# A graph network on one core: the row-by-row tile in five steps of sixteen instead of one of four, and the loads of the node windows addressed in bytes

## The reference

```
h = x @ enc_W + enc_b
for l in range(3):
    cat = concat([h[src], h[dst], edge_attr_16])
    m = relu(cat @ msg_W1[l] + msg_b1[l]) @ msg_W2[l] + msg_b2[l]
    agg = segment_sum(m, dst, num_segments=12500)
    h = gru_cell(agg, h, ...)
out = layernorm(x + relu(h @ ro_W1 + ro_b1) @ ro_W2 + ro_b2)
```

## Time and profile before

| what | value |
|---|---|
| runs of the kernel | 9832.15, 9768.75, 9798.1 us; median 9798.1 |
| the profiled execution's own time | 9777.42 us |
| its span from first to last instruction | 9775.6 us |
| busy: POOL / DVE / PE / ACT | 4639.2 / 3532.6 / 2880.1 / 346.4 us |
| granted TensorE clock, mean | 0.571 of full speed |
| rows issued one by one at L473 | 9792 on SP, 9792 on ACT |
| gathers at L798 | 4767 (and 63 more at other lines) |

### The profile page before, as it was taken

One profiled execution on the slowest core, in us unless ns is written; L12 is line 12 of the kernel. 1 busy time (PEld: TensorE's weight loads), 2 busy tenths in 40 slices (PEclk: granted clock), 3 DMA queues, 4 the chain that ended last, 5 costly groups with the idle time before them and its releaser, 6 DMA issues.

```text
span 9775.6 us, 72182 instructions
## 1 busy us (share of the span) xinstructions
PE 2880.1 (29%) x7290; PEld 1610.2 (16%) x7290; DVE 3532.6 (36%) x4656; ACT 346.4 (4%) x542; POOL 4639.2 (47%) x4865
## 2 busy tenths in 40 slices
PE   3323322322322332222222222223232222322223
PEld 2111111111111221111111111112111111111112
DVE  2333333333333433333333333333333334333334
ACT  0000000000000000000000000000000000000001
POOL 5444444444444454444444444445454445545543
PEclk6555555555555555555555555555555555555555
DMA  3111111111111111111111111111111111111111
GB/s 87 31 31 30 30 30 30 28 31 30 31 30 30 30 28 30 30 30 30 30 30 29 30 30 27 30 31 30 30 31 31 30 30 34 31 31 31 31 30 25
DMA packets 351443, 308.63 MB, mean 32 GB/s; under 512 B 149364, under 2 KB 237518, under 8 KB 350568
## 3 DMA queue, kind: packets, MB, share of 16 engines
q0 software_dynamic: 155328, 159.79, 8.6%
q1 hardware_dynamic: 118271, 110.17, 4.0%
q10 hardware_dynamic: 77328, 33.96, 1.4%
HBM read 280.52 MB, written 22.83 MB: 31 GB/s over the span
## 4 chain that ended last, share of the span: by engine, by line
SPq 57%; issue 38%; DVE 2%; PE 1%; another core or an unknown queue 1%; DMA 0%; ACT 0%; POOL 0%; DVEq 0%; ACTq 0%; POOLq 0%
SPq L473 46%; SPq L469 6%; SPq L642 2%; SPq L633 1%; SPq L527 1%; DVE work_ps L1493 1%; SPq L630 1%; DVE folds L1528 0%; DVE p_src L1490 0%; PE bank L838 0%; DMA p_src<-p_tab 0%; PE work_ps L949 0%; PE bank L962 0%; SPq L662 0%
## 5 line engine op out<-in xcount | busy, mean ns | idle before, releaser
L798 POOL DMA_INDIRECT p_src<-p_tab,idx_all x4767 | 4551.1, 955 | 4916.8 <-DVE work_ps L1493 3467.4
L962 PE MATMUL bank<-hot,folds 128*128 128x96 f32 x2496 | 660.1, 413 | 4012.9 <-issue 2053.0
L1490 DVE TENSOR_TENSOR p_src<-work_ps,p_src 128x512 f32<-128x512 f32 x624 | 427.6, 685 | 3374.9 <-DMA p_src<-p_tab 2912.1
L962 PEld LDWEIGHTS bank<-hot,folds 128*128 128x128 f32 x2496 | 532.1, 296 | 4278.5 <-issue 2198.0
L949 PE MATMUL work_ps<-w_edges,msg 128*128 128x512 f32 x1248 | 1120.0, 997 | 21.4 <-DMA windows_sb<-q_tab 21.4
L1523 DVE SCALAR_TENSOR_TENSOR work_ps<-work_ps,rel 128x1024 f32<-128x1024 f32 x624 | 768.8, 1232 | 21.5
L1493 DVE TENSOR_TENSOR work_ps<-p_src,bank 128x1024 f32<-128x1024 f32 x624 | 767.0, 1229 | 21.4
L1528 DVE TENSOR_REDUCE folds<-work_ps 128x256 f32<-128x1024 f32 x624 | 758.4, 1215 | 0.0
L959 PE MATMUL bank<-hot,counts 128*34 128x96 bf16 x416 | 68.9, 261 | 2248.6 <-issue 1278.6
L1538 DVE TENSOR_TENSOR sums<-bank,sums 128x96 f32 x624 | 158.1, 253 | 872.6 <-remote 699.5
L959 PEld LDWEIGHTS bank<-hot,counts 128*34 128x34 bf16 x416 | 27.1, 108 | 2368.2 <-issue 1359.8
(11 more groups left out here) (167 smaller groups left out, 1800.9 us busy)
## 6 DMA issues: line engine op xcount, KB each, us to landing
p_src<-p_tab ACTq DMA_DIRECT2D x9792, 0.2 KB
p_src<-p_tab SPq DMA_DIRECT2D x9792, 0.2 KB
p_src<-p_tab,idx_all POOLq DMA_INDIRECT x4830
msg<-in_edge_k SPq DMA_DIRECT2D x156, 256.0 KB
pick<-rel_tab SPq DMA_DIRECT2D x312, 96.0 KB
windows_sb<-q_tab ACTq DMA_DIRECT2D x312, 24.0 KB
windows_sb<-q_tab SPq DMA_DIRECT2D x312, 24.0 KB
pick<-q_tab ACTq DMA_DIRECT2D x312, 24.0 KB
```

Of the source, the lines that this page charges most:

```text
L798: pool.indirect_dma_start(out=p_src[r][0:rows, t, :], out_offset=None, in_=p_tab[l][0:NODES, :], in_offset=bass.IndirectOffsetOnAxis(ap=id ...
L962: last = nc.tensor.matmul(fold_ps, folds[:, b, :], hot_all[n % 2][:, s * BLOCKS + b, 1:WINDOW + 1], start=(b == 0), stop=(b == BLOCKS - 1))
L1490: nc.vector.tensor_tensor(rows, edge_ps[k % 2], rows, ALU.add).then_inc(with_edge, 1)
```

## The change

What it does, in four parts. (1) `SINGLE_STEPS` lists the steps whose last tile is loaded row by row, in all layers alike: of every 16 steps those with m % 16 in (3, 6, 9, 12, 15), without the last step, 64 a layer. POOL gathers 7 tiles there. (2) Rows on SP and ACT are issued in pieces of 16, ordered by a due time `max(5 * m - 25 + 4 * q, 0)` in fifths of a step (there are 64 entries, so `every` is 4): SP puts the pieces due before 5(4g-6) ahead of the inputs of group g, ACT those due in [5m, 5m+5) at step m. (3) In layer 0 the shift of a chunk's counts and the load of chunk nodes come one group later, behind the first piece of rows of that group. (4) DVE makes byte offsets of the window starts once (two small operations before the first step), SP and ACT load those, and a window's address needs no register operation.

```diff
+SINGLE_STEPS = [[m for m in range(STEPS - 1) if m % 16 in (3, 6, 9, 12, 15)]] * LAYERS
+SINGLE_ROWS = SINGLE_STEPS[0]
+SINGLES = len(SINGLE_ROWS)
...
-        def has_singles(m):
+        def has_singles(l, m):
 
-            return m % GROUP == GROUP - 1 and m // GROUP < SINGLES
+            return m in SINGLE_STEPS[l]
...
-        def pieces_at(m):
-
-            due = [(m + AHEAD_OF - q, q) for q in range(PIECES)]
-            if m == 0:
-                due = [(GROUP - 1, q) for q in range(PIECES) if GROUP - 1 + q <= AHEAD_OF]
-            return [(at, q) for at, q in due if at < STEPS and has_singles(at)]
+        def pieces_between(l, a, b):
+
+            every = 5 if len(SINGLE_STEPS[l]) < STEPS // 4 else 4
+            return [(m, q) for m in SINGLE_STEPS[l] for q in range(PIECES) if a <= max(5 * m - 25 + every * q, 0) < b]
+
+        def held_behind(g):
+
+            return pieces_between(0, 5 * (GROUP * (g - 1) - 6), 5 * (GROUP * g - 6))[0]
...
+        def group_starts(kind, g, b):
+
+            return nc.values_load_multi_w_load_instructions(
+                first_bytes[b][0:1, GROUP * g:GROUP * (g + 1)], engines=(kind,), ...)[1]
+
+        def window_rows(l, start):
+
+            here = q_tab[l].bitcast(U8).rearrange("n b -> (n b)")[bass.ds(start, ROW_BYTES)]
+            return bass.AP(here.tensor, here.offset, [[ROW_BYTES, REACH], [1, 2 * ROW_BYTES]])
...
                     for g in range(2, GROUPS):
-                        single_rows(sp, mybir.EngineType.SP, l, GROUP * (g - 2) + GROUP - 1, 0, SP_ROWS, sp_singles)
+                        for m, q in pieces_between(l, 0 if g == 2 else 5 * (GROUP * (g - 1) - 6), 5 * (GROUP * g - 6)):
+                            single_rows(sp, mybir.EngineType.SP, l, m, PIECE * q, PIECE, sp_singles)
+                            if l == 0 and g > 2 and g % 2 == 0 and (m, q) == held_behind(g):
+                                shift_counts(g // 2 - 2)
+                                chunk_nodes(g // 2)
                         group_inputs(n0 + g, g)
                         group_windows(l, n0 + g, g)
...
-                        if l == 0 and g % 2:
-                            shift_counts(g // 2 - 1)
-                            chunk_nodes(g // 2 + 1)
...
-                        for at, q in pieces_at(m):
+                        for at, q in pieces_between(l, 5 * m, 5 * m + 5):
...
+                for b in range(2):
+                    nc.vector.tensor_scalar(first_bytes[b], base_i[:], float(ROW_BYTES), float(b * AHEAD * ROW_BYTES), ALU.mult, ALU.add)
```

More of the change, by code:

```diff
@@ L71 @@
 PIECES = 4
-AHEAD_OF = 5
 PIECE = (128 - SP_ROWS) // PIECES
 SINGLE_SEMS = 4
-SINGLES = GROUPS - 1
+SINGLE_STEPS = [[m for m in range(STEPS - 1) if m % 16 in (3, 6, 9, 12, 15)]] * LAYERS
+SINGLE_ROWS = SINGLE_STEPS[0]
+SINGLES = len(SINGLE_ROWS)
 PAIRS = CHUNKS // 2
@@ L173, in build @@
         p_src = [p_src_all[:, s] for s in range(GATHER_SLOTS)]
+        first_bytes = [spread[:].bitcast(I32), late[:].bitcast(I32)]
         dst_steps = sums[0:STEPS // 2, ENC_PAIRS * CHUNK:ENC_PAIRS * CHUNK + 2 * STEP].bitcast(I32).rearrange("p (j e) -> p j e", j=2)
@@ L191, in build @@
         both = pre_all[:].rearrange("p s g f -> p (s g f)")
-        raw_nodes = zr[0:GROUPS, 0:128].bitcast(I32)
-        offsets = p_src[ROW_SLOTS].rearrange("p t f -> p (t f)")[0:GROUPS, 0:128].bitcast(I32)
+        raw_nodes = zr[0:SINGLES, 0:128].bitcast(I32)
+        offsets = p_src[ROW_SLOTS].rearrange("p t f -> p (t f)")[0:SINGLES, 0:128].bitcast(I32)
         src_seen = [dst_flat[:, 0:STEP], both[0:LATE_ROWS, :].bitcast(I32)]
@@ L451, in build, with gathers_of @@
         late_ps = [zr_ps[:], n_ps[:]]
-        def gathers_of(m):
-            return LAST_TILES if m == STEPS - 1 else EDGE_TILES - has_singles(m)
-        def has_singles(m):
-            return m % GROUP == GROUP - 1 and m // GROUP < SINGLES
+        def gathers_of(l, m):
+            return LAST_TILES if m == STEPS - 1 else EDGE_TILES - has_singles(l, m)
+        def has_singles(l, m):
+            return m in SINGLE_STEPS[l]
         def single_rows(eng, kind, l, m, first, n, landed):
@@ L467, in single_rows @@
             for at in range(first, first + n, PIECE):
-                here = offsets[m // GROUP:m // GROUP + 1, at:at + PIECE]
+                here = offsets[SINGLE_ROWS.index(m):SINGLE_ROWS.index(m) + 1, at:at + PIECE]
                 starts = nc.values_load_multi_w_load_instructions(
@@ L474, in single_rows @@
                                   table[bass.ds(start, ROW_BYTES)].unsqueeze(0)).then_inc(landed[nth_single(l, m) % SINGLE_SEMS], 16)
-        def pieces_at(m):
-            due = [(m + AHEAD_OF - q, q) for q in range(PIECES)]
-            if m == 0:
-                due = [(GROUP - 1, q) for q in range(PIECES) if GROUP - 1 + q <= AHEAD_OF]
-            return [(at, q) for at, q in due if at < STEPS and has_singles(at)]
+        def pieces_between(l, a, b):
[3 more added lines that the diff above has]
+            return pieces_between(0, 5 * (GROUP * (g - 1) - 6), 5 * (GROUP * g - 6))[0]
         def nth_single(l, m):
-            return l * SINGLES + m // GROUP
+            return sum(len(SINGLE_STEPS[j]) for j in range(l)) + SINGLE_STEPS[l].index(m)
         def chunk_stages(m):
@@ L523, in results_of @@
             return (bank[0] if c == LOOPS else n_ps)[0:SPANS[c][1], 0:SPANS[c][2] * HID]
+        def group_starts(kind, g, b):
+            return nc.values_load_multi_w_load_instructions(
+                first_bytes[b][0:1, GROUP * g:GROUP * (g + 1)], engines=(kind,), min_val=b * AHEAD * ROW_BYTES, max_val=(NODES + b * AHEAD) * ROW_BYTES,
+                skip_runtime_bounds_check_because="base_i is a destination, at most NODES, and a row is as long as the factor")[1]
+        def window_rows(l, start):
+            here = q_tab[l].bitcast(U8).rearrange("n b -> (n b)")[bass.ds(start, ROW_BYTES)]
+            return bass.AP(here.tensor, here.offset, [[ROW_BYTES, REACH], [1, 2 * ROW_BYTES]])
         def group_bases(eng, kind, g):
@@ L636, in group_windows @@
             def group_windows(l, n, g):
-                bases = group_bases(sp, mybir.EngineType.SP, g)
+                starts = group_starts(mybir.EngineType.SP, g, 0)
                 for j in range(GROUP):
-                    here = q_tab[l][bass.ds(bases[j], REACH), :]
-                    pairs = bass.AP(here.tensor, here.offset, [[HID, REACH], [1, PAIR]])
-                    sp.dma_start(windows_of[GROUP * (n % 2) + j][0:REACH, 0:PAIR], pairs).then_inc(edges_in[n % 2], 16)
+                    sp.dma_start(windows_of[GROUP * (n % 2) + j][0:REACH, 0:PAIR].bitcast(U8), window_rows(l, starts[j])).then_inc(edges_in[n % 2], 16)
             def shift_counts(c):
@@ L690, in _ @@
                             fast_rows(g // 2 - 1)
-                        if l == 0 and g % 2:
-                            shift_counts(g // 2 - 1)
-                            chunk_nodes(g // 2 + 1)
-                    single_rows(sp, mybir.EngineType.SP, l, STEPS - 1 - GROUP, 0, SP_ROWS, sp_singles)
+                    for m, q in pieces_between(l, 5 * (GROUP * (GROUPS - 1) - 6), 5 * STEPS):
+                        single_rows(sp, mybir.EngineType.SP, l, m, PIECE * q, PIECE, sp_singles)
+                        if l == 0 and (m, q) == held_behind(GROUPS):
+                            shift_counts(GROUPS // 2 - 2)
+                            chunk_nodes(GROUPS // 2)
                     if l == 0:
@@ L749, in _ @@
             for m in range(PRE):
-                for t in range(gathers_of(m)):
+                for t in range(gathers_of(0, m)):
                     pool.indirect_dma_start(
@@ L787, in _ @@
                         if early(l, m):
-                            for t in range(gathers_of(m)):
+                            for t in range(gathers_of(l, m)):
                                 pool.indirect_dma_start(
@@ L802, in _ @@
                 for m in range(PRE):
-                    pool.wait_ge(ahead[m], 16 * gathers_of(m))
+                    pool.wait_ge(ahead[m], 16 * gathers_of(0, m))
                 pool.wait_ge(idx_first_in, 16)
@@ L1181, in windows_ahead @@
             def windows_ahead(l, n, g):
-                bases = group_bases(act, mybir.EngineType.Activation, g)
+                starts = group_starts(mybir.EngineType.Activation, g, 1)
                 for j in range(GROUP):
-                    here = q_tab[l][bass.ds(bases[j] + AHEAD, REACH), :]
-                    pairs = bass.AP(here.tensor, here.offset, [[HID, REACH], [1, PAIR]])
-                    act.dma_start(windows_of[GROUP * (n % 2) + j][REACH:ROWS, PAIR:2 * PAIR], pairs).then_inc(ahead_in[n % 2], 16)
+                    act.dma_start(windows_of[GROUP * (n % 2) + j][REACH:ROWS, PAIR:2 * PAIR].bitcast(U8), window_rows(l, starts[j])).then_inc(ahead_in[n % 2], 16)
             with act.If(slow == 0):
@@ L1473, in landed @@
             def landed(k):
```

(8 more changed lines are left out.)

## The result

The changed kernel takes 10488.59 us (median of 4 runs, 10478.5 to 10492.36) against 9799.74 us before: 1.071 times the time, 95% interval 1.0685 to 1.0735. Forecast were 10620 us and a range of 10280 to 11600. The profiled execution has a span of 10476.7 us, 701 more than before; forecast were 845 more.

What follows compares the result with a forecast made beforehand. SyncE's issuing of rows was taken as the bound. From 9777 us profiled, +1031 for more rows, -41 for fewer gathers, -120 for the shift and -25 for byte offsets gave 10622, predicted as 10620 us, range 10280 to 11600.

Steps and rivals of the forecast that it cites:

- What bounds the kernel: SyncE's queue: its issuing of rows one by one bounds the kernel; GpSimd is held back by VectorE, which waits for rows.
- More rows, fewer gathers: SyncE: 2496 more rows at the fast pace, 0.413 us each, +1031 us; 39 fewer gathers on GpSimd, -41 us.
- The mean price during gathers: SyncE's mean time per row while GpSimd gathers, taken as unchanged at 2.06 us; 1.6 would give +650, 2.47 +1190 us.
- The balance of 16 steps: 250.7 us now: gathers 156, inputs and windows 20, remaining 74.5 hold 180 rows at 0.413; changed kernel 276.4 us.
- The shift: Layer 0, SyncE's stall before shifting the counts: moving it behind a piece of rows saves 120 us, bounds 0 and -240.
- Byte offsets: SyncE's window loads: one register operation fewer for each of 624 windows, -25 us, bounds 0 and -95.
- rival (d): Shared descriptor generator: with SyncE and ScalarE always issuing together, a row costs 0.463 us, +1156, total 10747; chance 0.05.
- (a): VectorE's release of slots to GpSimd: gather bursts become short, rows go out cheaply during gathers, 8510 us; chance 0.07.
- (b): ScalarE's chunk stages, delayed by its extra rows, hold VectorE and come onto the path: +967, 11590 us; chance 0.11.
- (c): SyncE's slow pace belongs to rows, not gathers: each new row costs 0.909 us, 11900 us in all; chance 0.05.
- (e): Nothing moves: extra rows fit where the slow pace lifts, the mean during gathers falls to about 1.13, 9780 us; chance 0.04.
- the signs named: Expected in the changed profile: SyncE gapless, VectorE waiting in nearly all 192 steps, paces near 0.41 and 2.5, steps 16.6-17.3 us.

Runs made afterwards that it cites:

- the old density: Changed kernel with rows one by one in steps m % 4 == 3 again, 51 tiles a layer; 9615.82 us, 0.9854 of the kernel before (slow pace), 1.0000 (even pace).
- Six of sixteen: Changed kernel with row-by-row steps m % 16 in (3, 5, 8, 11, 13, 15), 77 tiles a layer; 11349.1 us, 1.1602 of the kernel before.

## Why the prediction was right, point by point

**What bounds the kernel.** Right: chain, waits and the gapless issuing are SyncE's in the changed kernel too, and removing ScalarE's rows changes nothing.

**More rows, fewer gathers.** Right in kind, a fifth too large. Forecast +1031 - 41 = +990. By the ratios the changed kernel stands at 10489 and the one with the old density at 0.9854 x 9799.74 = 9657: +832, give or take some 30 us by the two intervals, so 0.33 us a row net of the gathers. The two profiled executions differ by 898 us (10476.7 less 9578.8). Six of sixteen gives +868 for the next 39 tiles. The mis-sized term rests on a pitch (start to start) of 0.413 us from one window. Over all rows that go out clear of the gathers the pitch is 0.412 us before, 0.409 with the old density and 0.403 in the changed kernel. On the changed kernel's 8,700 such rows the 0.006 us between the last two are an estimated 50 of the 158 us; the rest I can't place.

**The mean price during gathers.** Taken as unchanged, and it is, but at another level. The balance of 16 steps booked as rows the stalls at the shift and the 300 us of the span that lie outside the three stretches of the earlier trace rows, so it found only 76 rows during gathers, at 2.06 us each. Counted in the traces, from 5 us after the start of each burst to 5 us after its end, 91 of 256 rows go out during gathers in the kernel before, 95 of 256 with the old density and 92 of 320 in the changed kernel: 1.69, 1.62 and 1.65 us a row. Nor did the bursts change as forecast. The 31 gathers of the earlier trace rows were not the usual burst: of 256 before, 96 had 23 gathers, 98 had 8 and 50 had 31; of 244 now, 143 have 23. That the mean price stayed is what the sum needed; it had been assumed, not worked out, and so held partly by luck.

**The shift.** Right: forecast -120, with -125 from the stall alone; with the old density layer 0 lost 151 us, and 33 and 7 of such a loss have other causes, as layers 1 and 2 show: 118 to 144 us, from one execution of each. In the changed kernel the wait is gone, and layer 0 is now the quickest.

**Byte offsets.** Forecast -25, bounds 0 and -95. Alone they were only timed where SyncE isn't the bound (1.0000); in the slow pace they are within the 40 us above.

**The lock, and rival (d).** The Trainium skill (Perfetto Trace Analysis, section "DMA Instruction — HWDGE (DVE, Sync)") has the shared generator locked until all descriptors are made. Both engines' instructions last 0.463 us together and SyncE keeps 0.402 us a row with ScalarE issuing: the full-length lock is not seen. SyncE's pace during gathers with ScalarE silent is 2.28 us, not half of 2.47. Rival (d)'s own price, +1156 for the rows, is further off than the forecast's.

**The rivals.** (a) short bursts: no, the usual burst is 29 us. (b) ScalarE's stages: VectorE's wait for its tanh is 404.7 us for 381.5 before, that for its sigmoid 177.9 for 293.1, and SyncE waits for PE's mixing once. (c) the price as a mean over all rows: no, 0.33 us and not 0.909. (e) no. Of the signs named, a step was to take 16.6 to 17.3 us and takes 16.3 to 16.5; VectorE waits for rows 171 times, not in all 192; the slow pace is 2.00 us in the window shown, for 2.5; the waits before the shift are gone as forecast.

**What it left out.** I took the two paces of the earlier trace rows as this kernel's nature. They come with the chip: on others the same gathers don't slow SyncE, the bound is GpSimd and the change is worth -0.5%, so that there the forecast of +8% would have had the wrong sign. It came out because the result was timed at the pace at which its rows had been read. No rival said so, though rows of before hinted at it: the same instruction lasted 228 ns in the median and 1477 ns at most, and 153 tiles loaded by hand cost far more time than the gathers they save.

## What to carry to other kernels

A row of 256 bytes issued by hand costs its queue 0.32 to 0.41 us at best and several times that where gathers slow the issuing engines; it pays only while the issuing engine has time to spare, and one gather saved is worth 1.26 us for 64 such issues on each of two queues. Before tuning such a balance, time a version without it: 6345 and 7547 us without rows, against 6155 and 9800 with them, would have shown that with the rows the kernel is 3% faster on one kind of chip and takes 30% longer on the other. And take known stalls out of a balance before reading a price from its remainder.

## What the runs showed of the hardware that was not expected

Chips differ in how gathers by GpSimd act on the other engines' issuing (or their states do, as said above). On some, a transfer instruction of SyncE never lasts over 0.533 us and rows keep 0.39 us each during gathers; on others the row's move and its transfer each last up to 1.4 us and more while GpSimd gathers, 1.65 us a row on the mean, and the same kernel takes 9800 instead of 6155 us. GpSimd's own gathers keep 1.26 us on both. With rows removed the ratio shrinks to 7547 against 6345, and of what is left most that can be named lies on VectorE's two register-addressed additions (1314.5 and 646.9 us of "remote"). SyncE is slowed no less when ScalarE issues no rows: 1.93 us a row on the mean during gathers, counted as above, for 1.69. What in the chip makes the difference stays open; nothing was tried on it beyond these runs.
